# Three unread identity products ahead of each of the last nine state updates

## The reference

```
def step(S, qkv):
    qt, kt, vt = qkv
    S = S + LR * jnp.einsum('bd,be->de', vt, kt)
    out = jnp.einsum('de,be->bd', S, qt)
    return (S, out)
```

## Time and profile before

| | before |
|---|---|
| median of three runs | 243.22 us |
| the profiled execution's own time | 244.94 us |
| its span | 243.1 us |
| TensorE busy | 217.7 us (90% of the span) |
| VectorE busy | 142.0 us (58%) |
| ScalarE busy | 140.2 us (58%) |
| GpSimd busy | 164.0 us (67%) |
| mean granted TensorE clock | 0.973 |

### The profile page before, as it was taken

One profiled execution on the slowest core, in us unless ns is written; L12 is line 12 of the kernel. 1 busy time (PEld: TensorE's weight loads), 2 busy tenths in 40 slices (PEclk: granted clock), 3 DMA queues, 4 the chain that ended last, 5 costly groups with the idle time before them and its releaser, 6 DMA issues.

```text
span 243.1 us, 4901 instructions
## 1 busy us (share of the span) xinstructions
PE 217.7 (90%) x1560; PEld 190.9 (79%) x1560; DVE 142.0 (58%) x594; ACT 140.2 (58%) x328; POOL 164.0 (67%) x142
## 2 busy tenths in 40 slices
PE   0399996998999999999999899999999999999660
PEld 0389894876889899888988788999988988977430
DVE  1749962453267477946588726627777534464462
ACT  6012101454536767767667758577667767798650
POOL 1058978899657799929999659629998531542221
PEclk9999999999999999999999999999999999999955
DMA  6999929726163237564372733432433343344344
GB/s 183 378 431 423 416 101 217 303 65 217 40 190 91 54 83 234 131 200 99 89 234 64 245 97 80 108 94 73 99 95 79 96 99 77 87 111 121 91 109 110
DMA packets 30143, 37.15 MB, mean 153 GB/s; under 512 B 4039, under 2 KB 26877, under 8 KB 29862
## 3 DMA queue, kind: packets, MB, share of 16 engines
q1 hardware_dynamic: 29708, 36.46, 50.3%
q10 hardware_dynamic: 410, 0.38, 0.4%
HBM read 19.77 MB, written 5.92 MB: 106 GB/s over the span
## 4 chain that ended last, share of the span: by engine, by line
PE 47%; POOL 21%; DMA 17%; DVE 7%; issue 4%; ACT 2%; SPq 0%; POOLq 0%; DVEq 0%; ACTq 0%
PE conv L434 17%; POOL scaled L345 13%; DMA rows<-x_windows 11%; PE vr_ps L473 7%; PE state_ps L480 7%; PE out L495 7%; DMA mixed<-values 6%; PE state_ps L483 5%; POOL g_low L891 3%; POOL ln_rstd L902 2%; POOL rho L897 2%; PE turn L465 2%; DVE scaled L345 2%; PE conv L440 1%; ACT state L605 1%
## 5 line engine op out<-in xcount | busy, mean ns | idle before, releaser
L434 PE MATMUL conv<-scaled,wt 128*128 128x256 f32 (+3 forms) x460 | 119.9, 370 | 10.0 <-DMA wt<-weight 10.0
L345 POOL TENSOR_TENSOR scaled<-rows,gam 128x832 f32<-128x832 f32 x60 | 94.0, 1583 | 3.3 <-PE conv L434 2.0
L434 PEld LDWEIGHTS conv<-scaled,wt 128*128 128x128 f32 x460 | 75.5, 194 | 13.5 <-DMA wt<-weight 10.0
L600 ACT ACTIVATE values<-vr_ps,rho 128x256 f32<-128x256 f32 x85 | 40.3, 474 | 33.0 <-PE vr_ps L473 30.7
L891 POOL TENSOR_TENSOR g_low<-g_t,g_high 128x512 fp32r<-128x512 f32 (+1 forms) x22 | 27.1, 1234 | 38.5 <-ACT g_high L587 38.5
L715 DVE SCALAR_TENSOR_TENSOR images<-out,rho,images 128x128 f32<-128x128 f32 (+1 forms) x85 | 28.4, 336 | 37.7 <-PE out L495 32.0
L605 ACT COPY state<-state_ps 128x256 f32<-128x256 f32 x85 | 31.7, 373 | 20.5 <-PE state_ps L483 18.8
L613 ACT ACTIVATE images<-images,ln_shift,ln_gain 128x128 f32<-128x128 f32 x81 | 36.9, 484 | 8.0 <-DVE ln_shift L747 8.0
L480 PE MATMUL state_ps<-mixed 128*128 128x128 f32 x170 | 36.6, 298 | 4.2 <-DMA mixed<-values 3.4
L480 PEld LDWEIGHTS state_ps<-mixed 128*128 128x128 f32 x170 | 29.3, 191 | 13.0 <-issue 6.7
L693 DVE BATCH_NORM_STATS2 ln_stats<-images 128x6 f32<-128x128 f32 x85 | 18.6, 280 | 31.7 <-ACT images L594 31.7
(11 more groups left out here) (106 smaller groups left out, 232.2 us busy)
## 6 DMA issues: line engine op xcount, KB each, us to landing
rows<-x_windows SPq DMA_DIRECT2D x13, 864.0 KB, 5.8
mixed<-values SPq DMA_DIRECT2D x170, 64.0 KB, 2.0
out<-images SPq DMA_DIRECT2D x42, 128.0 KB, 2.4
images<-x_rows SPq DMA_DIRECT2D x3, 624.0 KB, 21.7
images<-x_rows SPq DMA_DIRECT2D x1, 1456.0 KB, 13.0
images<-x_rows SPq DMA_DIRECT2D x1, 1248.0 KB, 15.5
images<-x_rows SPq DMA_DIRECT2D x1, 832.0 KB, 19.6
small<-smalls SPq DMA_DIRECT2D x1, 512.0 KB, 8.6
```

The costliest lines, as they stand in the source:

```text
L345: return eng.tensor_tensor(scaled[:, s, at:at + N], window, gains, ALU.mult)
L434: last = pe.matmul(conv_ps[g % 2][:, at:at + n * B], wt[:, s], scaled[:, s, a % RING:a % RING + n], start=first, stop=(g < EARLY and s == ...
L600: act.activation(values[:, t % VALUE_SLOTS].rearrange("p a e -> p (a e)"), vr_ps[:, 0:2 * E], ACT.Identity, scale=rho[:, t + 1:t + 2]).the ...
```

## The change

A new helper issues three products of the identity with itself, in f32, into conv_ps[1]. Nothing reads them. TensorE issues them ahead of the update in each of the steps 76 to 84, nine times, so 27 products in all. Ahead of the first, TensorE waits until ScalarE has copied the last group out of the convolution's banks. The products themselves wait for nothing and signal nothing.

```
+FILL_FROM = TILES - 9
+FILL = 3
...
+            def fill():
+
+                for _ in range(FILL):
+                    pe.matmul(conv_ps[1][:, 0:E], small[:, IDENT], small[:, IDENT], start=True, stop=True,
+                              skip_group_check=True)
+
             def step(t):
                 g, i = t // PER_GROUP, t % PER_GROUP
+                if t == FILL_FROM:
+                    pe.wait_ge(g_ready, GROUPS)
+                if t >= FILL_FROM:
+                    fill()
                 if t >= 0:
                     update(t)
```

## The result

The changed kernel takes 245.52 us, the median of four executions from 245.29 to 245.97; the kernel before takes 243.3 beside it. The ratio is 1.0101, with a 95% interval from 1.0074 to 1.0128. The ratio is not the quotient of the two medians: by the medians the change costs 2.2 us in both series, by the ratios 2.5 and 1.9. Three executions of the kernel before, of 246.66 to 248.39 us, lie over 1.5% above its fastest and are in none of these figures. The forecast was 244.9 with a range from 242.9 to 246.4, and 0.63 for slower.

What follows compares the result with a forecast made beforehand. TensorE's chain of updates and reads was taken to bound the tail: +2.32 us to update 80, -1.17 idle time, -0.35 behind update 81, giving +0.8. Between 244.0 and 245.7 the middle, 244.9, was taken; range 242.9 to 246.4.

Steps and rivals of the forecast that it cites:

- The product's price: On TensorE, one f32 identity product takes 0.22 us at full clock, three take 0.66, all 27 take 5.9.
- Exposed behind reads, partly hidden ahead of the others: TensorE's steps from update 76: odd ones, products behind reads, grow to 2.21 us; even ones go from 1.17 to 1.45.
- The tail: TensorE from update 76's products to the last read: read ends at 236.16 against 235.38, 0.8 us later.
- steps 77 and 79: Odd TensorE steps whose second tile's reads wait for the state: 1.17 + 0.38 + 0.66 = 2.21 us, gaps about 0.5.
- Transfers: Transfers to mixed have 2 us of slack in the changed kernel, so neither late transfer nor 1.81 us issue matters.
- The clock holds to the last read: TensorE's largest gaps from update 76 are about 0.5 us, so full clock lasts to the last read.
- From the profiled execution to the median: Whole kernel: profiled 244.94 us against median 243.22, a 1.72 difference; changed kernel 244.0 to 245.7, middle 244.9 taken.
- The upper end: Whole kernel: if the tail explains the 1.72 us between profile and median, the changed kernel stays at 245.7 (+2.5).
- the best case that was worked out: Kernel before without the late transfer (0.79 us) and the clock's fall (1.67): 244.94 - 2.46 = 242.48 us.
- A: Rival: TensorE's product costs less, three take 0.33 us; last read 1.0 earlier, 242.2 us; chance of faster 0.12.
- B: Rival: timed runs are like the profile, whole kernel +0.8 us, 244.0 or less, within 0.5%; chance 0.25.
- D: Rival: TensorE's clock falls anyway at 229.9, last read ends 4.0 us later, 247.2 us; chance 0.08.

Runs made afterwards that it cites:

- both series: Changed kernel timed twice against the kernel before: 245.52 us against 243.3 (ratio 1.0101), then unedited again 245.71 against 243.54 (ratio 1.0078).
- the second trace of before: Profile of the kernel before run again with no edit: traced execution 244.19 us, median of that run 244.11 us, ratio 1.0021.

## Why the prediction was right

**The product's price** was 0.22, and is (six take 1.33). **Exposed behind reads, partly hidden ahead of the others**: the steps were forecast as 1.45 and 2.21 and are 1.48 and 2.21 to 2.27; step 82 as 1.17, and is 1.12. The tail would by the forecast be 234.86 + 0.49 + 0.44 - 219.73 = 16.06; three traces have 16.27. Of the missing 0.2 half is in the first products, which take 219.71 - 218.94 = 0.77 and not 0.66, since they come behind reads. The forecast counted from the start of the first products 16.4 us to the last read's end and 7.7 behind it; these are 16.7 and 7.8. Products in the waits alone cost nothing over the kernel before, those behind the reads alone 1.3 us.

**Right in size, not in cause: steps 77 and 79.** The forecast let the reads wait for the state in every odd step, 1.17 + 0.38 + 0.66 = 2.21. In 81 and 83, which have no vr, the chain does go through ScalarE's copy. In 77 and 79 nothing waits for the state: update 0.44, vr 0.35, the reads of both tiles 0.59 and products 0.86 fill TensorE, 2.25 us from update to update. The gaps of about 0.5 us that were forecast there don't exist. That the two sums are so close is luck; with six products it makes no difference, with one it does (above).

**Transfers.** As forecast, none matters in the changed kernel. They didn't go away: in its first trace one issue of SyncE took 1.73 us, and the slowest transfer to mixed from 216 us on landed after 3.2 us. No update waited for it.

**The clock holds to the last read**: it does in the traces, and no execution of the changed kernel has a mean under 0.987. That it is the products that hold it is not shown: with the stores moved it holds without them.

**From the profiled execution to the median.** This was the open step, with 244.0 at one end, 245.7 at the other, and the middle taken for lack of a reason. The upper end was true, and the stated 244.9 was short by 0.6 to 0.8. The profile of before was an execution like the 21 in 114 with a mean clock under 0.976, and these are 1.6 us slower than the 69 at 0.983 and more, where 1.67 was worked out as what the full clock gives back. How the 1.6 divide between the clock and the late transfers that come with it, these runs don't say: the two go together. The changed kernel has no such spread, so the loss against the usual execution is 2.1 to 2.2, and against the profiled one 0.35. That the upper end, 244.94 + 0.8 = 245.7, is met so closely is in part luck: up to add_out the changed kernel lost 1.09 and not 0.8, and the profile of before had come to step 76 some 0.4 us later than the mean of the 13 traces (219.37), which makes up for it. The fastest of the three runs (242.46) and the best case that was worked out (242.48) had pointed to it.

**The rivals.** A (a product is half as dear) is out by the rows with six. B (+0.8) would need executions like the profiled one, and these are a minority (21 of 114). D (the clock falls anyway, 247.2) came in no execution.

**What stays open.** Why a transfer to mixed sometimes lands after 3.4 us and not 2.0. The stores have a part in what it costs, since moving two of them brings 0.9 us; but the late transfer of the first trace (issued at 224.24) has two others between it and the store at 221.56, and with the stores moved one issue of 1.42 us stood in the queue too. How an execution of before with the usual time spends its tail wasn't traced.

## What to carry to other kernels

Work that is put into an in-order queue to keep a clock is free only where the queue waits for something that is still to come; behind the last instruction that had to wait (here the reads of the newest state) it delays the next link of a recurrence by its full length. Price it for each place in the queue, and leave it out of the places behind the wait. Before a clock loss in one profile is paid for, ask in how many executions it happens, and whether what emptied the engine, here late transfers in a queue that also issues the stores, can be taken away instead. And ask what comes next: here, 0.6 us behind a shorter tail, VectorE.

## What the runs showed of the hardware

- Single transfers in SyncE's busy queue land late: in the traces of before after 3.74 and 3.43 us where the median is 2.0. All 13 traces have one between 216 and 236 us, of 2.7 to 3.7 us, whether an update waits for it or not. In 11 of them one issue to mixed took 1.2 to 2.0 us (1.81 in the first trace of before, 1.42 with the stores moved) where its neighbours took 0.60.
- The granted clock outlasted a wait of 0.98 us, and a wait of 1.73 us that ended at 233.13 was followed by its fall between 234 and 235, in the second trace of before (the clock is 0.85):

```profile
234.00:235.00 1.00, 0.43 (x2) 0.19 (x2) 0.47 (x3) 1.00 (x4) 0.00 (x0) 0.85 0.05 12
```

- One execution of the kernel with products ahead of the last four updates took 451 us: TensorE's matmuls took 640 ns each on line 438 instead of 370, and the added products near the end 455 ns instead of 283, while the trace recorded a granted clock of 1.00. The other 23 executions took 243.3 to 245.1.

```profile
L438 PE MATMUL conv<-scaled,wt 128*128 128x256 f32 (+3 forms) x460 | 229.8, 640 | 9.9 <-DMA wt<-weight 9.9
```
